# Second graph attention on one core: edge lists in rings of four steps, one flat loop on TensorE

## The reference, cut to what matters

```
loop = arange(n);  src = concat(edge_index[0], loop);  dst = concat(edge_index[1], loop)
h = (x @ W).reshape(n, 4, 64)
a_src = einsum("nhc,hc->nh", h, att_src);  a_dst = einsum("nhc,hc->nh", h, att_dst)
e = leaky_relu(a_src[src] + a_dst[dst], 0.2)
ex = exp(e - m[dst])                         # m: a maximum per destination
out = segment_sum(ex * h[src], dst) / segment_sum(ex, dst)
return relu(out + bias)                      # added to x
```

## Time and profile before

| | us |
|---|---|
| median of 3 runs (lowest, highest) | 3318.38 (3304.72, 3322.56) |
| profiled execution, own time | 3312.67 |
| its span, first to last instruction | 3310.6 |
| changed part, first to last instruction (874.8 to 2428.9) | 1554 |
| mean granted TensorE clock, whole span | 0.770 of full speed |

### The profile page before, as it was taken

The page is one execution under the profiler, slowest core; times in us unless marked ns, Lnnn a source line. Parts: engine busy times, 40 slices in busy tenths (PEclk is TensorE's granted clock), DMA queues, the critical chain, the costliest instruction groups (busy, mean ns, idle before and its releaser), DMA issues. The chain is left out here.

```text
span 3310.6 us, 55683 instructions
## 1 busy us (share of the span) xinstructions
PE 2158.7 (65%) x13130; PEld 1965.5 (59%) x13131; DVE 1548.6 (47%) x4163; ACT 1006.1 (30%) x2712; POOL 1486.7 (45%) x1459
## 2 busy tenths in 40 slices
PE   6232259984466655656755656655654299999997
PEld 4132258873355554555654555555543299999997
DVE  5564435657334433433433433433445345556454
ACT  3132246663210111111111111111134266665664
POOL 1456634440255555555555545545525524334233
PEclk9655579997667767766767767767755599999999
DMA  6212233325333233233223323323333423333331
GB/s 177 62 55 66 73 114 106 110 93 188 93 82 78 76 79 79 76 79 78 76 79 78 79 73 79 79 77 80 79 98 125 137 42 89 46 66 85 48 68 25
DMA packets 232367, 279.34 MB, mean 84 GB/s; under 512 B 102963, under 2 KB 186526, under 8 KB 232086
## 3 DMA queue, kind: packets, MB, share of 16 engines
q0 software_dynamic: 82160, 200.19, 22.9%
q1 hardware_dynamic: 149392, 77.86, 9.0%
q10 hardware_dynamic: 776, 0.89, 0.1%
HBM read 202.11 MB, written 78.46 MB: 85 GB/s over the span
## 5 line engine op out<-in xcount | busy, mean ns | idle before, releaser
L1700 POOL DMA_INDIRECT at_G<-h_as,at_idx x850 | 805.9, 948 | 735.2 <-issue 385.5
L1851 PE MATMUL at_pAgg<-at_G,at_OH 128*128 128x260 f32 x1700 | 504.6, 462 | 91.8 <-DVE at_ACC L1749 51.0
L1851 PEld LDWEIGHTS at_pAgg<-at_G,at_OH 128*128 128x128 f32 x1700 | 387.6, 235 | 176.6 <-issue 51.3
L1836 PE MATMUL at_pTr<-g_ident,at_OH 128*128 128x128 f32 x850 | 157.1, 332 | 477.7 <-ACT at_OT L1809 436.9
L1809 ACT ACTIVATE at_OT<-at_pTr 128x384 f32<-128x384 f32 (+1 forms) x300 | 131.4, 471 | 1102.8 <-remote 695.3
L1836 PEld LDWEIGHTS at_pTr<-g_ident,at_OH 128*128 128x128 f32 x850 | 120.9, 170 | 513.7 <-ACT at_OT L1809 448.7
L1415 ACT ACTIVATE e_full<-e_pH,g_bias_hidden 128x256 f32<-128x256 f32 x640 | 322.6, 504 | 96.4 <-PE e_pH L1320 60.7
L1223 POOL DMA_INDIRECT out_dram<-e_ob,e_to x108 | 171.0, 1584 | 401.9 <-DMA out_dram<-e_ob,e_to 190.8
L1844 PEld LDWEIGHTS at_pAd<-at_cur,at_OT 128*128 128x128 f32 x1700 | 320.4, 290 | 49.8 <-ACT at_OT L1809 49.8
L1720 DVE TENSOR_TENSOR at_Z<-at_G,at_pAd 128x24 f32<-128x24 f32 x150 | 26.1, 174 | 690.0 <-PE at_pAd L1844 592.0
L1844 PE MATMUL at_pAd<-at_cur,at_OT 128*128 128x8 f32 x1700 | 319.1, 326 | 37.9 <-ACT at_OT L1809 37.9
(11 more groups left out here) (307 smaller groups left out, 4089.3 us busy)
## 6 DMA issues: line engine op xcount, KB each, us to landing
e_xs<-slot_rows_e SPq DMA_DIRECT2D x55, 261.0 KB
e_xs<-slot_rows_e SPq DMA_DIRECT2D x54, 257.0 KB
at_G<-h_as,at_idx POOLq DMA_INDIRECT x850
b_rows<-expert_out SPq DMA_DIRECT2D x14, 896.0 KB, 7.3
g_raw_first<-in_L_ffn_W_dram POOLq DMA_DIRECT2D x8, 1024.0 KB, 8.1
g_raw_last<-in_L_ffn_W_dram POOLq DMA_DIRECT2D x8, 1024.0 KB, 6.3
xt_ar<-a_og SPq DMA_DIRECT2D x7, 910.0 KB, 4.5
h_as<-b_og SPq DMA_DIRECT2D x7, 910.0 KB
```

The source lines that it names most:

```text
L1700: gp.indirect_dma_start(G[j][:, c, :], None, K.T1, bass.IndirectOffsetOnAxis(ap=idx[j][:, c:c + 1], axis=0)).then_inc(gathered[j], 16)
L1836: last = nc.tensor.transpose(pTr[h][:, (c - a) * P:(c - a + 1) * P], OH[j][:, c, :], K.ident[:, :])
L1851: last = nc.tensor.matmul(pAgg[:, 0:DIM + 4], OH[j][:, c, :], G[j][:, c, :], start=(j == 0 and c == 0), stop=(j == NJ - 1 and c == CHUNKS[ ...
```

## The change

Four things change, all in `attention`:

- **Edge lists in rings.** A step's source ids are one transfer of 17 columns into slot s mod 4 of `edge_src`, the destination ids the same into `edge_dst` (two transfers a step for six). A ring slot's group is 6, 6 or 5 columns of the 17. After starting a step's two transfers, SP waits for both to land, and at a tile's end for the own rows. A last dummy transfer follows the final step.
- **Own rows in a ring** of four tiles, `own[:, t mod 4, :]`.
- **Source ids are copied.** ACT copies a group's ids from the ring into `idx[j]` (`keep_sources`), one step ahead, between its other work; POOL waits for that copy (`src_kept[j]`) where it waited for the transfer. The source ring's slot is free when group 2's copy is done, the destination ring's slot when group 2's one-hots are made, the own slot when DVE has used it.
- **One flat loop on PE.** PE no longer loops over tiles and reads no table in the loop. The wait for `cur_ready` is gone: DVE itself waits until `cur` is written before it makes the tile's first one-hots, on which PE waits anyway.

```diff
-OFFS = (0, 6 * P, 12 * P)
+OFFS = (0, 6, 12)
+ALL = sum(CHUNKS)
+DEPTH = 4
...
-        dcol = [sb(f"dcol{j}", [P, CHUNKS[j]]) for j in J]
+        edge_src = sb("edge_src", [P, DEPTH, ALL], I32)
+        edge_dst = sb("edge_dst", [P, DEPTH, ALL])
...
-        own = sb("own", [P, DIM + 4])
+        own = sb("own", [P, DEPTH, DIM + 4])
...
-                    freed(sp, own_used, t)
-                    sp.dma_start(own[:, :], K.T1[bass.ds(r0, P), :]).then_inc(own_in, 16)
+                    place = sp.snap(t % DEPTH)
+                    sp.wait_ge(own_used, t + 1)
+                    sp.sem_inc(passed, 1)
+                    sp.dma_start(own[:, bass.ds(place, 1), :].rearrange("p o c -> p (o c)"), K.T1[bass.ds(r0, P), :]).then_inc(own_in, 16)
...
-                        at = [sp.snap(e0 + OFFS[j]) for j in J]
-                        for j in J:
-                            ne = CHUNKS[j] * P
-                            freed(sp, scored[j], s)
-                            sp.dma_start(idx[j][:, :], K.SRCP[bass.ds(at[j], ne)].rearrange("(p c) -> p c", p=P)).then_inc(src_in[j], 16)
-                            freed(sp, onehots[j], s)
-                            sp.dma_start(dcol[j][:, :], K.DSTP[bass.ds(at[j], ne)].rearrange("(p c) -> p c", p=P)).then_inc(dst_in[j], 16)
+                        slot = sp.snap(s % DEPTH)
+                        landed = sp.snap(s * 16 + 16)
+                        sp.wait_ge(src_kept[NJ - 1], s + 1)
+                        sp.sem_inc(passed, 1)
+                        sp.dma_start(edge_src[:, bass.ds(slot, 1), :].rearrange("p o c -> p (o c)"),
+                                     K.SRCP[bass.ds(e0, SE)].rearrange("(p c) -> p c", p=P)).then_inc(src_in, 16)
+                        sp.wait_ge(onehots[NJ - 1], s + 1)
+                        sp.sem_inc(passed, 1)
+                        sp.dma_start(edge_dst[:, bass.ds(slot, 1), :].rearrange("p o c -> p (o c)"),
+                                     K.DSTP[bass.ds(e0, SE)].rearrange("(p c) -> p c", p=P)).then_inc(dst_in, 16)
+                        sp.wait_ge(src_in, landed)
+                        sp.wait_ge(dst_in, landed)
+                        sp.sem_inc(passed, 1)
+                    sp.wait_ge(own_in, sp.snap(t * 16 + 16))
+                    sp.sem_inc(passed, 1)
...
             def _(gp):
-                        gp.wait_ge(src_in[j], s * 16 + 16)
+                        gp.wait_ge(src_kept[j], s + (1 + (DEPTH if j == NJ - 1 else 0)))
...
             def _(v):
-                    V.tensor_copy(cur[:, :], adm[:, bass.ds(t, 1), :].rearrange("p o k -> p (o k)")).then_inc(cur_ready, 1)
-                    ch.settle()
+                    ch.link(V.tensor_copy(cur[:, :], adm[:, bass.ds(t, 1), :].rearrange("p o k -> p (o k)")))
...
+                v.sem_inc(own_used, DEPTH)
+                v.sem_inc(onehots[NJ - 1], DEPTH)
...
             def _(act):
+                def keep_sources(s, j):
+                    slot = act.snap(s % DEPTH) if not isinstance(s, int) else s % DEPTH
+                    act.wait_ge(src_in, s * 16 + 16)
+                    act.sem_inc(passed, 1)
+                    nc.scalar.activation(idx[j][:, :], edge_src[:, bass.ds(slot, 1), OFFS[j]:OFFS[j] + CHUNKS[j]].rearrange("p o c -> p (o c)"),
+                                         ACT.Copy).then_inc(src_kept[j], 1)
...
                     exps(s, 0)
+                    keep_sources(ahead, 0)
                     keep_turned(s, 2)
                     exps(s, 1)
+                    keep_sources(ahead, 1)
                     exps(s, 2)
+                    keep_sources(ahead, 2)
...
             def _(pe):
-                with pe.Fori(0, TILES) as t:
-                    n, s0 = tile_steps(pe, t)
-                    pe.wait_ge(cur_ready, t + 1)
-                    pe.sem_inc(passed, 1)
-                    with pe.Fori(0, n) as g:
-                        s = pe.snap(s0 + g)
+                n, s0 = tile_steps(pe, TILES - 1)
+                with pe.Fori(0, pe.snap(s0 + n)) as s:
...
```

More of the change, by code:

```diff
@@ L1639, in attention @@
         init = sem("init")
-        src_in = [sem(f"src_in{j}") for j in J]
-        dst_in = [sem(f"dst_in{j}") for j in J]
+        src_in = sem("src_in")
+        dst_in = sem("dst_in")
+        src_kept = [sem(f"src_kept{j}") for j in J]
         gathered = [sem(f"gathered{j}", software=True) for j in J]
@@ L1657, in attention @@
         NJ = len(CHUNKS)
[L1658 to L1659 removed]
+        lifts = (acc_done, ot_ready, *scored, *onehots[0:NJ - 1], *agg_done)
+        START, STEP, END = 3, 3 * NJ, 5
         def tile_steps(eng, t):
@@ L1680, in _ @@
                                                 "a step begins before its tile's last edge, and SE edges of padding follow the last")
-                        at = [sp.snap(e0 + OFFS[j]) for j in J]
-                        for j in J:
-                            ne = CHUNKS[j] * P
-                            freed(sp, scored[j], s)
-                            sp.dma_start(idx[j][:, :], K.SRCP[bass.ds(at[j], ne)].rearrange("(p c) -> p c", p=P)).then_inc(src_in[j], 16)
-                            freed(sp, onehots[j], s)
-                            sp.dma_start(dcol[j][:, :], K.DSTP[bass.ds(at[j], ne)].rearrange("(p c) -> p c", p=P)).then_inc(dst_in[j], 16)
+                        slot = sp.snap(s % DEPTH)
[13 more added lines that the diff above has]
+                    sp.sem_inc(passed, 1)
+                n, s0 = tile_steps(sp, TILES - 1)
+                s = sp.snap(s0 + n)
+                slot = sp.snap(s % DEPTH)
+                sp.wait_ge(src_kept[NJ - 1], s + 1)
+                sp.sem_inc(passed, 1)
+                sp.dma_start(edge_src[:, bass.ds(slot, 1), :].rearrange("p o c -> p (o c)"),
+                             K.SRCP[EDGES:EDGES + SE].rearrange("(p c) -> p c", p=P)).then_inc(src_in, 16)
                 K.clear_last(sp)
@@ L1708, in one_hots @@
                     c = CHUNKS[j]
-                    v.wait_ge(dst_in[j], s * 16 + 16)
+                    slot = v.snap(s % DEPTH)
+                    if j == 0:
+                        v.wait_ge(dst_in, s * 16 + 16)
                     freed(v, agg_done[j], s)
-                    V.tensor_tensor(OH[j][:, :, :], dcol[j][:, :].rearrange("p (c o) -> p c o", o=1).to_broadcast([P, c, P]),
+                    at = edge_dst[:, bass.ds(slot, 1), OFFS[j]:OFFS[j] + c].rearrange("p o c -> p (o c)")
+                    V.tensor_tensor(OH[j][:, :, :], at.rearrange("p (c o) -> p c o", o=1).to_broadcast([P, c, P]),
                                     TI.rearrange("p (o n) -> p o n", o=1).to_broadcast([P, c, P]),
@@ L1772, in tile @@
                         finalize(ch, t - 1)
+                    own_t = own[:, bass.ds(t % DEPTH if isinstance(t, int) else v.snap(t % DEPTH), 1), 0:DIM].rearrange("p o c -> p (o c)")
                     ex_t = exs[:, bass.ds(t, 1), :].rearrange("p o h -> p (o h)")
@@ L1817, in exps @@
                                          ACT.Exp).then_inc(ex_ready, 1)
+                def keep_sources(s, j):
[4 more added lines that the diff above has]
+                                         ACT.Copy).then_inc(src_kept[j], 1)
+                act.sem_inc(src_kept[NJ - 1], DEPTH)
+                for j in J:
+                    keep_sources(0, j)
                 n, s0 = tile_steps(act, TILES - 1)
-                with act.Fori(0, act.snap(s0 + n)) as s:
+                total = act.snap(s0 + n)
+                with act.Fori(0, total) as s:
+                    ahead = act.snap(s + 1)
                     keep_turned(s, 0)
@@ L1830, in turn @@
                 def turn(s, j):
-                    freed(pe, onehots[j], s + 1)
+                    pe.wait_ge(onehots[j], s + (2 if j < NJ - 1 else 1 + DEPTH))
                     for h, (a, z) in enumerate(((0, 3), (3, CHUNKS[j]))):
@@ L1853, in aggregate @@
                     last.then_inc(agg_done[j], 1)
[L1855 to L1870 removed]
+                n, s0 = tile_steps(pe, TILES - 1)
+                with pe.Fori(0, pe.snap(s0 + n)) as s:
+                    turn(s, 0)
+                    turn(s, 1)
+                    destinations(s, 0)
+                    destinations(s, 1)
+                    freed(pe, acc_done, s)
+                    aggregate(s, 0)
+                    turn(s, 2)
+                    destinations(s, 2)
+                    aggregate(s, 1)
+                    aggregate(s, 2)
 _INS = ['x', 'src', 'dst', 'L0_gnn_weight', 'L0_gnn_attn_l', 'L0_gnn_attn_r', 'L0_ffn_router_w1', 'L0_ffn_router_b1',
```

15 lines of the change are left out of this document (2 added, 13 removed).

## The result

The changed kernel takes 3358.16 us (median of 6, 3339.99 to 3376.77) against 3315.31 for before on the same chip: ratio 1.0144, 95% interval 1.0117 to 1.017. The forecast was 3303. The profiled execution took 3339.99 us, the shortest of the six, span 3338.1, first to last gather 883.85 to 2437.17 us (before 881.19 to 2411.70).

What follows compares the result with a forecast made beforehand. Bound: the chain from the release of PE's held signals through A0 to the next gather. Rings -20, copies +0.5, first step +4 sum to -15.5: 3297 us profiled, 3303 on the median; likeliest case 3288 to 3318, range 3110 to 3630.

Steps and rivals of the forecast that it cites:

- if the hold keeps its place: PE's signals stay held while a gather stream runs and are let go 2.3 us after its last gather; chance 0.42.
- rival B: A2's signal slips through, POOL runs all 17 gathers in one stream; 36.9 us a step, +300 us, 3620; chance 0.22.
- rival C: Hold starts earlier and catches A1, POOL pauses after six gathers; about 26.8 us a step, -196 us, 3122; chance 0.13 with mixes.
- 12 + 5: A step's gathers on POOL: twelve in one stream, a pause, five more; forecast to stay, at 30.4 us a step.
- E's 32.4: Rival: PE's transposes pass too, destinations are held, DVE's scores wait; 32.4 us a step, +79 us, 3397; chance 0.08.
- F: Rival: the hold goes and POOL's 17 gathers are the bound; 21.3 us a step, -461 us, 2857; chance 0.08.
- Rings, -0.40 us a step: POOL's wait for ids goes, A0's signal is next in line; 0.40 us a step over 49 steps, -20 us.
- Copies on ACT: Three a step, 0.6 us, hidden in ACT's waits; 29 us without that cover; +0.5 us once at the start.
- Flat loop: PE's first transpose could come 0.27 us earlier, but its result is held: gain 0; up to 13 us without the hold.
- First step, +4: SP fills the rings during the first stream, which may start the hold earlier: +8 us once or 0, half taken.

Runs made afterwards that it cites:

- lists_in_stream_2: The changed kernel with SP's source ids also waiting for group 2's scores of four steps earlier, so they start within a gather stream; 3325.72 us, 0.994 of before on chip C.
- the pin: Group 1's gathers also wait for the step before's A2, in each kernel: before 3169.73 us (0.956), changed 3148.75 us (0.948), both against before on chip B.

## Why the prediction was wrong

**The step that failed** is the premise of the sum, "if the hold keeps its place". The prediction saw that nearly all of SP's transfers would leave the streams and wrote "What that does to the hold no row shows; see the rivals"; the forecast then went on as if it did nothing. The prediction gave the premise 0.42, with no row behind it. It did not hold. In the streams of 17 A2's signal comes mostly 11.4 to 13.5 us in, where in before it came near 17.0, and so it is there when the 13th gather asks for it, 15.06 us in: rival B's mechanism, in 31 of 49 streams. In 16 others A1's signal comes too late for the seventh gather: rival C's. Only two are 12 + 5, where the forecast had all. Both signs came in one run, and their mix differs from chip to chip. In the traced execution on A the loss is mostly what is left of +86 and -55 us, not a cost of the added work, which E bounds at 0.3%. lists_in_stream_2 ties this to SP's order, the part that the prediction left unpriced: with the lists back in the stream the old pattern returns in all but three steps.

The prediction also had A2 end 7.5 us into the stream; in the streams of 17 it ends 9.0 to 9.4 us in (the 22 matmuls of A1 and A2 take 6.78 us for 5.09), and its signal is out earlier all the same.

**The rivals' prices.** B was put at 36.9 us a step and took 34.0, because the hold was taken to last until 2.3 us after the stream; in a stream of 17 the signals trickle out within it (ACT's first copy 13.5 us in). C was put at 26.8 and took 25.8; its mechanism was right, with A0's signal 25.1 us in for 26. E's 32.4 did not appear as a kind of its own. F, no hold, was put at 2857 and given 0.08: chips D, E and F are that case for both kernels, 2784 to 2789. It is worth more than forecast since other stages are shorter too: of the 529 us between before on A and on D, the 50 steps can be given about 459 (1530.5 us from first to last gather on A, 1071.0 for after on E); the rest is outside them. It is no effect of the change.

**Rings, -0.40 us a step.** The reading was right that 7.03 us of waiting for ids were not 7 us of gain, that A0 is next in line, and that the pause would be about 6.6: 6.85. Its size was not refuted where the premise held: with 12 + 5 back in place lists_in_stream_2 is 16.8 us below before on C (0.994, 0.991 to 0.996), where the sum had 15.5. That can't be split by step, since before was not traced on C, and the run has one more wait than the changed kernel; its step of 30.7 us can be set only beside before's 30.8 on A. With the pin both kernels step at 27.3. Without the hold POOL alone sets the step, and rings can gain nothing (1.0015, 1.000 to 1.003).

**Copies on ACT.** 0.2 us each and hidden: the ratio on E bounds all added work of the change at 0.3%, with 21.4 us a step set by POOL alone.

**Flat loop.** Put at nothing, or a gain of 13 us without the hold. Where there is no hold the whole change gains nothing. Where it is, the loop alone stands at 1.004 (1.000 to 1.008).

**First step, +4.** The second stream starts 25.0 us after the first, 24.87 before: nothing.

**What the hold is** stays open. The trace of after on A has 20,354 semaphore updates and on E 37,280, for the same 55,760 instructions: where the hold is, almost half of them are missing (40% in before on A). The Trainium skill ("NOTIFIC — the notification-queue block", section "7.1 Overflow: three behaviours, one of which stalls the engine") says that the block's inner pipeline holds producers back rather than lose a record, and that a full queue either drops records or stalls who writes them. Missing records, late signals and SP's instructions 0.7 us apart, all on the same chips, fit that; no run here shows the queue itself. Nor is it shown why three chips have it and three do not.

**Why a kind repeats itself** is argued only. The seventh gather could start 7.53 us into a stream. In after's 6 + 11 steps A1's signal, where the trace has it, comes 7.8 to 8.6 us in, and POOL pauses; in the streams of 17 it comes 7.0 to 7.3 us in, and POOL runs on. After a 6 + 11 the next stream begins 2.9 us behind eleven gathers, after a 17 it begins 12.7 us behind. What makes a series end was not tried.

## What to carry to other kernels

Where signals reach other engines late and in bursts, a change that moves no work can still move the time by several per cent either way, through which signal gets in before a queue runs on; compare how long the unbroken runs of gathers are before and after, and not only totals of waits. Before any verdict on such a kernel run both on several chips: here one chip said +1.4%, the next -4.0%, a third 0. Where a sum holds only under a premise ("the hold keeps its place") and a part of the change touches that premise (here the moved transfers), the premise needs a row or a run of its own before the sum becomes the forecast. And of two kernels whose patterns differ from chip to chip, a trace on one chip says little about a trace on another.

## What the runs showed of the hardware

- PE's signal of A2 came 9 to 10 us late in most steps of before on A; on E every signal of PE that the trace has of this stage came 0.01 us after the modelled end. The kernel before takes 3315 to 3342 us on the three chips with late signals and 2784 to 2787 on the three others.
- A long stream of gathers is not enough for it: 850 in a row, 1.26 us each, held nothing on E.
- Where it is, SP is slow as well: the same kernel's SP instructions within a stream stand 0.71 us apart on C and 0.09 on D (median).
- With SP's list transfers and the instructions around them put into every stream, A2's signal came 17 us in on C and 46 of 49 steps were 12 + 5; in single streams of the changed kernel two transfers did not do that.
- One added wait on POOL gave 4.4% (before) and 5.2% (after) against before on B; on E, where signals are prompt, it cost 2.0%.
